# A two-layer attention and mixture-of-experts kernel on one core: masks of single-head maxima on VectorE, layer 0's gates inside its expert loop, eight output buffers, V's padding and layer 1's first transposes at other places

## The reference, cut to what matters

```python
x = x + _layernorm(_L0_attn_ref(_layernorm(x), ...))   # 16 heads of 16, causal, biases
x = x + _layernorm(_L0_ffn_ref(_layernorm(x), ...))    # 32 experts of 192, top 4, a shared expert
x = x + _layernorm(_L1_attn_ref(_layernorm(x), ...))   # 16 heads of 16, causal, rotary embedding
x = x + _layernorm(_L1_ffn_ref(_layernorm(x), ...))    # 32 experts of 176, top 4, capacity 128, shared expert of 704
```

## Time and profile before

| | |
|---|---|
| median of three runs | 754.69 us (753.72 to 756.21) |
| the profiled execution | 756.23 us, of which the span from first to last instruction is 754.5 us |
| mean granted clock of PE | 0.948 of full |
| busy PE, DVE, ACT, POOL | 671.9, 477.3, 322.4, 262.9 us |
| chain that ended last | PE 71%, DVE 20%, DMA 3%, issue 2%, ACT 2% |

### The profile page before, as it was taken

How to read it: one execution, slowest core, us unless ns; L and a number is a source line. 1 busy time by engine, 2 the same in 40 slices (tenths; PEclk the granted TensorE clock), 3 DMA queues, 4 the chain that set the end, 5 groups by cost and what they waited for, 6 DMA issues and landing times.

```text
span 754.5 us, 13333 instructions
## 1 busy us (share of the span) xinstructions
PE 671.9 (89%) x4388; PEld 441.6 (59%) x4388; DVE 477.3 (63%) x1264; ACT 322.4 (43%) x680; POOL 262.9 (35%) x308
## 2 busy tenths in 40 slices
PE   3988999999668999999975888999998899999991
PEld 2633444435447999999963533444444456999970
DVE  4588788864582444444475788788865785343457
ACT  2554666673133333222242533666664231433322
POOL 4140112111156676444431183112211203677621
PEclk9999999999679999999996979999999999999995
DMA  3534210070018999999770345002000630489762
GB/s 101 144 124 140 64 36 2 1 231 23 28 51 298 301 323 313 313 312 311 263 244 0 107 125 161 16 16 104 2 1 2 205 98 18 144 285 313 236 204 97
DMA packets 60294, 108.60 MB, mean 144 GB/s; under 512 B 11194, under 2 KB 37131, under 8 KB 60100
## 3 DMA queue, kind: packets, MB, share of 16 engines
q1 hardware_dynamic: 52532, 93.86, 37.9%
q0 software_dynamic: 7632, 13.86, 5.7%
q10 hardware_dynamic: 64, 0.03, 0.0%
HBM read 79.98 MB, written 19.79 MB: 132 GB/s over the span
## 4 chain that ended last, share of the span: by engine, by line
PE 71%; DVE 20%; DMA 3%; issue 2%; ACT 2%; POOL 1%; SPq 1%; ACTq 0%; DVEq 0%; POOLq 0%
PE ps L1156 17%; PE ps L983 9%; PE ps L901 8%; PE ps L969 7%; DVE mx L1622 6%; PE ps L1169 5%; PE ps L1171 5%; PE ps L1015 4%; PE ps L1095 3%; PE ps L853 3%; PE ps L1127 2%; DVE X L2014 2%; PE ps L904 2%; PE ps L934 1%; DMA outs<-X,token 1%
## 5 line engine op out<-in xcount | busy, mean ns | idle before, releaser
L1622 DVE TENSOR_REDUCE mx<-ps 128x1 f32<-128x512 f32 (+3 forms) x304 | 184.6, 656 | 37.8 <-PE ps L904 18.3
L1324 ACT ACTIVATE X<-ps 128x1024 f32<-128x1024 f32 (+1 forms) x192 | 147.5, 809 | 84.7 <-PE ps L969 84.4
L901 PE MATMUL ps<-KA,QA 112*128 112x512 bf16 (+3 forms) x384 | 118.4, 345 | 7.4 <-DVE mx L1622 3.3
L780 POOL DMA_INDIRECT outs<-X,token x95 | 94.9, 999 | 77.0 <-DVE X L1994 61.9
L748 POOL TENSOR_SCALAR_AFFINE_SELECT X<-X 128x512 f32<-128x512 f32 x64 | 40.7, 637 | 208.3 <-ACT X L1324 208.3
L1156 PE MATMUL ps<-QA,KA 128*128 x756 | 95.9, 277 | 2.6 <-issue 2.2
L969 PE MATMUL ps<-QA,KA 114*128 114x512 bf16 (+3 forms) x384 | 95.0, 330 | 2.6 <-ACT X L1324 1.2
L1981 DVE TENSOR_TENSOR X<-ps,X 128x128 f32<-128x128 f32 x95 | 27.7, 291 | 108.2 <-ACT X L1441 108.0
L1156 PEld LDWEIGHTS ps<-QA,KA 128*128 128x128 f32 x756 | 93.0, 193 | 4.8 <-issue 3.0
L901 PEld LDWEIGHTS ps<-KA,QA 112*128 112x128 bf16 x384 | 37.7, 100 | 85.2 <-DVE mx L1622 54.8
L772 POOL DMA_INDIRECT V<-token_rows,row_of_slot x64 | 65.6, 1025 | 57.1 <-DVE row_of_slot L1895 31.5
(11 more groups left out here) (304 smaller groups left out, 869.2 us busy)
## 6 DMA issues: line engine op xcount, KB each, us to landing
KA<-in_ex SPq DMA_DIRECT2D x95, 512.0 KB
X<-in_dn SPq DMA_DIRECT2D x95, 64.0 KB
outs<-empty SPq DMA_DIRECT2D x4, 1024.0 KB, 8.5
V<-outs SPq DMA_DIRECT2D x4, 1024.0 KB, 7.9
QA<-X SPq DMA_DIRECT2D x28, 128.0 KB, 2.5
KA<-X SPq DMA_DIRECT2D x28, 128.0 KB, 2.5
QA<-w_sdn SPq DMA_DIRECT2D x28, 128.0 KB, 2.5
KA<-parts_k SPq DMA_DIRECT2D x28, 128.0 KB, 2.4
```

Of the source, the lines that this page charges most:

```text
L780: pool.indirect_dma_start(out=outs[L], out_offset=bass.IndirectOffsetOnAxis(ap=token[L][:, i:i + 1], axis=0), in_=erows[:, g % OUT_RING, : ...
L901: mm = pe.matmul(ps[:, bank, j * w:(j + 1) * w], QA[0:KQ, h, i * P:(i + 1) * P], KA[0:KQ, h, s0:s0 + w], start=True, stop=not diag)
L1324: nc.scalar.activation(probs[:, st % PB, 2 * p:2 * p + 2, off:CH], ps[:, 4 + 2 * p:6 + 2 * p, off:CH], ACT.Exp, scale=SCALE).then_inc(S(f" ...
L1622: v.tensor_reduce(mx[:, part, i, h0:h0 + nh], ps[:, n % RB, 0:nh * w].rearrange("p (h w) -> p h w", h=nh), AX.X, ALU.max)\
```

## The change

Five edits:

1. `masked_by_dve`: in groups 1 to 3, a unit of a single head on the diagonal (384 or 512 keys, 16 a group, so 48 a layer and 96 in all) loses its mask matmul. DVE instead runs a `tensor_tensor_reduce` that adds `mask_wide` (zeros and then the mask, fp32, in a free part of xT) and takes the maximum; its sum goes as bf16 to one of two buffers in xT that nobody reads. It waits for the unit two before, which used the same buffer. POOL makes `mask_wide` once a layer at step 0.
2. `OUT_RING` 4 to 8, with `erows` in w_sgu in place of X.
3. Layer 0's gates move into its loop: ACT's Exp ahead of tile 48's Silu, `gates()` on DVE at tile 50, the 16 diagonals two a tile at tiles 52 to 59 (into xT). Behind the loop ACT runs one Exp on a [128, 1] tile.
4. POOL clears V's padding in two halves, ahead of its first and of its second root; ones and `bias_parts` wait until DVE has normalized tiles 4 to 7.
5. In layer 1, both halves are transposed ahead of the first q product, as in layer 0.

```diff
-OUT_RING = 4
+OUT_RING = 8
+GATES_IN_LOOP = 48
...
+def masked_by_dve(g, u):
+
+    _, i, _, nh, s0, w = MAX_UNITS[u]
+    return g > 0 and nh == 1 and s0 + w == (i + 1) * P
...
+        mask_wide = xT[:, 1, CH:T]
+        mask_sums = xT[:, 0, CH:T].bitcast(BF16).rearrange("p (r n) -> p r n", r=2)
...
-            for n in range(NC):
-                root(f"front{n}", rstd, TPC * n, TPC * (n + 1))
+            def v_rest(n):
+
+                return pool.memset(V[:, TPC * n:TPC * (n + 1), :, DH + 1:], 0.0)
+
+            ch.step(v_rest(0))
+            root("front0", rstd, 0, TPC)
+            ch.step(v_rest(1))
+            root("front1", rstd, TPC, NT)
...
-                    ch.link(pool.memset(V[:, :, :, DH + 1:], 0.0))
+                    ch.wait()
+                    pool.wait_ge(S("normed_dve"), DVE_NORMED["attention0"] + TPC)
...
+                    if st == 0:
+                        pool.wait_ge(S(f"qk_sb{L}"), 2 * KD * NC)
+                        pool.wait_ge(S(f"v_sb{L}"), NT)
+                        ch.step(pool.memset(mask_wide[:, 0:CH - P], 0.0))
+                        pool.tensor_copy(mask_wide[:, CH - P:CH], mask_q[:, :]).then_inc(S("mask_wide"), 1)
...
                 transposes(L, 0)
-                if L == 0:
-                    transposes(L, 1)
+                transposes(L, 1)
...
-                qk_unit(0)
-                if L == 1:
-                    transposes(L, 1)
-                for u in range(1, 4):
+                for u in range(4):
                     qk_unit(u)
...
-                                           KA[0:KQ, h, s0:s0 + w], start=True, stop=not diag)
-                            if diag:
+                                           KA[0:KQ, h, s0:s0 + w], start=True, stop=not diag or masked_by_dve(g, u))
+                            if diag and not masked_by_dve(g, u):
...
+                    if L == 0 and i == GATES_IN_LOOP:
+                        act.wait_ge(S("less_top0"), 1)
+                        nc.scalar.activation(gate[:, :, :], gate[:, :, :], ACT.Exp).then_inc(S("gate_exp0"), 1)
+                    if L == 0 and GATES_IN_LOOP + 4 <= i < GATES_IN_LOOP + 4 + 2 * K:
+                        if i == GATES_IN_LOOP + 4:
+                            act.wait_ge(S("gates"), 1)
+                        for x in range(2):
+                            diag_out((i - GATES_IN_LOOP - 4) // 2, (i - GATES_IN_LOOP) % 2 * 2 + x)
...
+                        if masked_by_dve(g, u):
+                            dve.wait_ge(S("mask_wide"), L + 1)
+                            dve.wait_ge(S(f"unit_out{L}"), EMPTIED[n][1] - 2)
+                            ins = v.tensor_tensor_reduce(mask_sums[:, u % 2, 0:w], ps[:, n % RB, 0:w], mask_wide[:, CH - w:CH], 1.0,
+                                                         -BIG, ALU.add, ALU.max, mx[:, part, i, h0:h0 + 1])
...
-                    if i == NTILE[L] + LAG - 2:
+                    if i == (GATES_IN_LOOP + 2, NTILE[1] + LAG - 2)[L]:
                         gates()
```

More of the change, by code:

```diff
@@ L393, in build @@
         KAf = KA[:, :, :].rearrange("p h t -> p (h t)").bitcast(F32)
-        erows = X[:, 0:OUT_RING * D].rearrange("p (r n) -> p r n", r=OUT_RING)
+        erows = w_sgu[:, :, :].rearrange("p k n -> p (k n)")[:, 0:OUT_RING * D].rearrange("p (r n) -> p r n", r=OUT_RING)
         rowsT_all = QAf.rearrange("p (k n) -> p k n", k=KD)
@@ L401, in rowsT, with gate_diag @@
             return rowsT_all[:, :, i * P:(i + 1) * P] if L == 0 else rowsT_ring[:, i % RING, :, :]
+        diag_early = xT[:, :, :].rearrange("p k t -> p (k t)")
         diags = (parts_k[:, :, :].rearrange("p r t -> p (r t)").bitcast(F32), X[:, 3072:3584])
-        def gate_diag(x, k):
+        def gate_diag(L, x, k):
             n = (K * x + k) * P
+            if L == 0:
+                return diag_early[:, n:n + P]
             return diags[0][:, n:n + P] if x < PARTS else diags[1][:, k * P:(k + 1) * P]
@@ L428, in build @@
         lane = sb("lane", [P, 1])
+        exp_ready = sb("exp_ready", [P, 1])
         minus_half = sb("minus_half", [P, NT])
@@ L452, in build @@
         used_f = X[0:1, 7888:7888 + OUT_RING]
-        used_rows = X[0:1, 7892:7892 + OUT_RING].bitcast(I32)
+        used_rows = X[0:1, 7896:7896 + OUT_RING].bitcast(I32)
         in_window = X[:, 7904:8160].rearrange("p (j n) -> p j n", j=QW)
@@ L1442, in e_silu, with diag_out @@
                                          ACT.Silu).then_inc(S("e_silu"), 1)
+                def diag_out(k, x):
+                    at = GATES_AT + k
+                    nc.scalar.activation(gate_diag(L, x, k), identf[:, :], ACT.Copy, scale=xn[:, ON_PE[L][x], at:at + 1])\
+                      .then_inc(S("gate_diag"), 1)
                 copied_to = 0
                 for i in range(NTILE[L]):
+                    if L == 0 and i == GATES_IN_LOOP:
[6 more added lines that the diff above has]
+                            diag_out((i - GATES_IN_LOOP - 4) // 2, (i - GATES_IN_LOOP) % 2 * 2 + x)
                     while copied_to <= min(copy_before(i), NROWT - 1):
@@ L1449, in _ @@
                     e_silu(i)
-                act.wait_ge(S(f"less_top{L}"), 1 + L)
-                nc.scalar.activation(gate[:, :, :], gate[:, :, :], ACT.Exp).then_inc(S(f"gate_exp{L}"), 1)
-                if L == 1:
-                    nc.scalar.activation(gall[:, :, :], gall[:, :, :], ACT.Exp).then_inc(S("gate_exp1"), 1)
-                act.wait_ge(S("gates"), L + 1)
-                for k in range(K):
-                    for x, i in enumerate(ON_PE[L]):
-                        nc.scalar.activation(gate_diag(x, k), identf[:, :], ACT.Copy,
-                                             scale=xn[:, i, GATES_AT + k:GATES_AT + k + 1]).then_inc(S("gate_diag"), 1)
+                if L == 0:
+                    nc.scalar.activation(exp_ready[:, :], lane[:, :], ACT.Exp, scale=0.0)
+                else:
+                    act.wait_ge(S("less_top1"), 2)
+                    nc.scalar.activation(gate[:, :, :], gate[:, :, :], ACT.Exp).then_inc(S("gate_exp1"), 1)
+                    nc.scalar.activation(gall[:, :, :], gall[:, :, :], ACT.Exp).then_inc(S("gate_exp1"), 1)
+                    act.wait_ge(S("gates"), 2)
+                    for k in range(K):
+                        for x in range(len(ON_PE[1])):
+                            diag_out(k, x)
                 if L == 1:
@@ L1621, in take_unit @@
                             dve.wait_ge(S(f"neg_max{L}"), PHASES.index((g - 1, part_chunk(u))) + 1)
-                        v.tensor_reduce(mx[:, part, i, h0:h0 + nh],
-                                        ps[:, n % RB, 0:nh * w].rearrange("p (h w) -> p h w", h=nh), AX.X, ALU.max)\
-                         .then_inc(S(f"unit_out{L}"), 1)
+                        if masked_by_dve(g, u):
[3 more added lines that the diff above has]
+                                                         -BIG, ALU.add, ALU.max, mx[:, part, i, h0:h0 + 1])
+                        else:
+                            ins = v.tensor_reduce(mx[:, part, i, h0:h0 + nh],
+                                                  ps[:, n % RB, 0:nh * w].rearrange("p (h w) -> p h w", h=nh), AX.X, ALU.max)
+                        ins.then_inc(S(f"unit_out{L}"), 1)
                         if u + 1 in CHUNK_UNITS:
```

2 lines of the change are left out of this document (1 added, 1 removed).

## The result

| | before | after |
|---|---|---|
| median, same chip | 754.59 us (8 runs, 752.05 to 757.45) | 748.37 us (8 runs, 745.22 to 751.7) |
| profiled execution, its span | 756.23, 754.5 us | 748.95, 747.2 us |
| mean granted clock of PE | 0.948 | 0.956 |
| chain: PE, DVE, DMA, POOL | 71%, 20%, 3%, 1% | 66%, 19%, 6%, 2% |

The ratio is 0.991, with a 95% interval from 0.9891 to 0.993: 6.2 us by the medians, 5.3 to 8.2 us by the interval. Forecast were 4.5 us and 750.2; sign and range hold. The terms hold less well: two of the four were too small, one is not there at all, and the masks gain more than forecast in one stretch and lose in another. From here on "lost" and "won" are against the kernel before.

A forecast was written before the change was run, and what follows sets the result against it. PE was taken to set the pace, DVE only at a few places. Masks 2.0, buffers and gates 0.8, padding 0.9, transposes 0.8 sum to 4.5 us: 754.69 to 750.2 us; forecast 747 to 752.3 (0.60), 8 in 10 746.0 to 756.5.

The forecast's parts named there:

- Masks: Both layers' attention: 4.2 us of masks leave PE's chain, less 1.9 and 0.3 for DVE, net 2.0 us gained.
- the price of the pair: DVE's second instruction in each masked unit: taken as 0.12 us, between 0.08 and 0.24.
- sixteen units and bursts: Attention, DVE's cost on the path: 8 masked units a layer, 1.9 us in all, plus 0.3 us (0 to 2) for bursts.
- POOL's tile: Ahead of POOL's first triangle: mask tile takes 0.5 us a layer, covered by PE's lag; uncovered 1.0 us in all.
- Eight buffers and early gates: End of layer 0's loop: copies no longer wait for scatters, planes start earlier; 0.8 us gained (0 to 2.1).
- what is late next is PE: Layer 0's end: DVE's statistics wait for PE's planes, so PE's step and DVE's little lag set the 0.8 us.
- V's padding: Layer 0's front: second transposes start 1.3 us sooner, 0.65 if the clock rises at the same instant; 0.9 us taken.
- Layer 1's transposes: Layer 1's front: second q product follows the first at once, 0.8 us gained (0.15 to 1.4, by the clock's rise).
- DVE's taking back: Rival, attention: at 0.24 us a unit the masks lose 1.6 us; 755.5 us; no change, 0.18 shared with another rival.
- the slow pair: Rival, attention: DVE becomes the bound, slower from 0.38 us a unit; at half rate 766.5 us; slower has chance 0.11.
- More: Rival: all upper bounds together, 9.3 us gained, 745.4 us; faster than the forecast range has chance 0.11.
- the things named as proof against: DVE never waiting for PE in 60-160 or 470-540 us, an up product delayed at tiles 48-52, first weighing waiting for POOL.

The follow-up runs named there:

- hoist_ring4: Changed kernel with SP loading the counts of used tiles inside layer 0's loop and four output buffers instead of eight: 747.64 us, ratio 0.9913 to the kernel before.
- hoist: Changed kernel with SP loading the eight counts of used tiles inside layer 0's loop instead of behind it: 745.91 us, ratio 0.9906 to the kernel before.
- masks_only: Kernel before with only the masks of single heads moved to DVE and POOL's mask tile: 750.15 us, ratio 0.9938 to the kernel before.
- after_again: The changed kernel itself, measured once more: 747.63 us, ratio 0.9921 to the kernel before.

## Why the prediction was right, and where not

The total lies in the range, and that is in part luck: the masks, the padding and layer 1's transposes won more than forecast (by 1.5, 1.4 and 0.4 us, as told below), the buffers less than nothing at their place, and part of what the masks won hangs on stretches of half clock that the prediction did not have.

- **Masks, predicted 2.0, measured 3.5 us alone.** Removing half of the masks from the chain was sized well (2.1 us a layer predicted, 2.3 in the earlier trace rows against after). The step that failed is the price of the pair: 0.12 us, with a bound of 0.08 from below, where 0.013 was measured. A lower bound was taken from the *duration* of a small instruction, though the durations of neighbours overlap, which the earlier trace rows had shown. So the 1.9 + 0.3 us for sixteen units and bursts are not there; DVE's share of the chain stays 4.5%. In their place stands something that the prediction did not have: up to 1.6 us a layer that a stretch of half clock costs once it lies behind the burst. The sign of "bursts" was right, the mechanism not. A second stretch of that kind is why the time is better than 2 x 1.86 less 1.27 and 1.20: before, it lies on the end of layer 1's attention (the window below), where all four traces with the masks on PE have one; of the ten with masks on DVE eight have none there and win another 1.6 us, which that of after loses again at 590 us. And from the last up product of layer 1 to the end of the program the four take 36.23 to 36.39 us, the ten 35.20 to 35.95, 0.7 us less by the means. 1.25, 1.6 and 0.7 are together about 3.5. That the last two follow from the masks is a tendency of 14 traces, and their cause is open.

```profile
574.00:577.00 3.00, 3.00 (x14) 1.89 (x17) 1.36 (x3) 1.02 (x1) 0.00 (x0) 0.50 0.00 0
```

- **POOL's tile, predicted hidden.** Not shown either way: 0.60 us in the chain of one trace, none in another of the same kernel.
- **Eight buffers and early gates, predicted 0.8 us.** The step that failed is "what is late next is PE". The counts that SP loads for each buffer were not costed: the edit doubles them, 2.4 us ahead of the loads. That was to be seen before the run, since the number of loads hangs on OUT_RING, and the trace of before has them on SP's queue. The prediction had the right condition, "0 if the planes land only just then", and even that was kind: 0.4 to 1 us lost in five of six traces. The mechanism is right where the loads are early: 1.42 us between hoist_ring4 and hoist, within its 0 to 2.1.
- **V's padding, predicted 0.9 us.** The second transposes follow the first directly, and the first product begins at 13.80 to 13.97 instead of 15.41 to 15.54, 1.6 us sooner. What failed is the halving for a clock that "rises at the same instant". The passes' own pace tells that it does not: in the chain sixteen took 7.87 us from 15.62 before, eight took 4.64 from 14.03 after. With 0.43 us for a fast pass (eight took 3.43 later on) and twice that for a slow one, 2.3 were slow before, until 17.6, and 2.8 after, until 16.4. The clock rose with the work, and more: the traces' first records of the granted clock, which begin with this rise, are at 17.5 us before and 16.3 after, as worked out, and over all traces at 13.98 to 16.31 us in the eleven with this edit and at 16.75 to 19.80 in the three without. (The windows read 1.00 ahead of the first record; the passes' pace says otherwise.) First maxima begin at 32.10 to 33.22 in the eleven traces with this edit, at 34.34 to 35.89 in the three without: 2.3 us between the means.
- **Layer 1's transposes, predicted 0.8 (0.15 to 1.4).** From the first transposes to the last pass of the second product, the three traces without the edit take 10.03 to 10.38 us, the eleven with it 8.13 to 9.69: 1.2 between the means. The mechanism is right, and the size was a little low. Not because the clock rose sooner, as the upper bound had it: masks_only and after_again both have the rise 7.7 us behind the first transposes and take 10.21 and 9.13, so at the same clock the closed gap is worth 1.1 us. The 1.9 us between before and after are that and an early rise.
- **The rivals.** DVE's taking back and the slow pair are out by the pitch of 0.48 and 0.61 us. "More" was the nearest, though not for its reasons. Of the things named as proof against, two came out: DVE without a wait for PE, but in the burst alone, where it had none in the kernel before either, and with 0.10 us of loss by the pairs; and the first weighing of layer 1 that waits for POOL.

The parts alone give 3.5 + 0.8 + 3.2 = 7.5 us by time, the whole 6.2; with over a microsecond of doubt on each that is no contradiction, and no interaction needs to be assumed.

## What to carry to other kernels

An instruction's duration is no price: take the pitch of neighbours, and where one of them is new, allow for its vanishing in its neighbour. When a ring grows, look for everything that is done once per slot on every queue; here the queue that only starts transfers paid 2.4 us at the one place where it was needed. And a stretch of low clock behind a burst belongs to the sum: work that is taken from PE where another engine sets the pace wins nothing and can move the slow stretch onto work that matters.

## What the runs showed of the hardware

- The read of DVE's accumulator is a row of 83 ns that adds 0.013 us to the pitch of its unit, and an fp32 SBUF source beside one in PSUM costs 2 ns at 512 columns (687 against 685).
- Where a stretch at 1.2 GHz lies differs with the work ahead of it and from one execution to the next: with the masks on PE the granted clock was 0.50 in the burst and 0.95 behind it, with the masks on DVE 1.00 and then 0.52, and in another execution of that same kernel the stretch lasted twice as long (58.8 to 65.6 us, where the first had 64.1 to 67.5). On up products one costs about 2 us; on a burst that DVE paces it cost nothing.
- The rise to 2.4 GHz in layer 1's front came 5.7 to 8.9 us behind the first transposes in the eleven traces in which that front's instructions are the same.
- Reading a value from SBUF into an SP register costs about 0.55 us with the instructions that belong to it, one after the other: 2.2 us for four, 4.5 for eight.
